# Graph kernel, edge part: the faded running total is written straight into the PSUM bank of the next sum

## The reference

```python
w_m = (efeat @ W_msg + b_msg).reshape(E, in_f, -1)      # E x 16 x 16
w_a = (efeat @ W_attn + b_attn).reshape(E, in_f, -1)
h_src = feat[src][:, :, None]
e1, e2 = w_m * h_src, w_a * h_src
seg_max = segment_max(e2, dst); ex = exp(e2 - seg_max[dst])
denom = segment_sum(ex, dst)
ft = segment_sum(e1 * (ex / denom[dst]), dst)
out = layernorm(x + ft.sum(axis=1))
```

## Time and profile before

| | us |
|---|---|
| median of 3 runs | 2380.55 |
| lowest, highest | 2374.79, 2388.63 |
| the profiled execution, device time | 2364.64 |
| its span, first to last instruction | 2362.8 |
| PE, DVE busy | 1745.0 (74%), 1722.0 (73%) |
| ACT, POOL busy | 1480.9 (63%), 1336.1 (57%) |
| mean granted clock of PE | 0.822 |

### The profile page before, as it was taken

How to read it: one execution, slowest core, us unless ns; L and a number is a source line. 1 busy time by engine, 2 the same in 40 slices (tenths; PEclk the granted TensorE clock), 3 DMA queues, 4 the chain that set the end, 5 groups by cost and what they waited for, 6 DMA issues and landing times.

```text
span 2362.8 us, 32949 instructions
## 1 busy us (share of the span) xinstructions
PE 1745.0 (74%) x5902; PEld 767.4 (32%) x5902; DVE 1722.0 (73%) x2102; ACT 1480.9 (63%) x5073; POOL 1336.1 (57%) x1556
## 2 busy tenths in 40 slices
PE   0566668950188888888878788888888888888845
PEld 0354442330033333333333333333333333333312
DVE  3576653120278898888879798889888888888956
ACT  5468830110367777777767677777777777777742
POOL 4234415445656666666666566666666666666640
PEclk9855569875589889888878898989888998889977
DMA  3010001001010000000000000000000000000000
GB/s 44 21 30 0 0 2 26 12 13 19 8 10 10 10 10 10 10 10 11 9 9 8 9 10 11 9 10 10 10 10 10 10 11 9 9 10 10 10 4 8
DMA packets 84286, 26.53 MB, mean 11 GB/s; under 512 B 62108, under 2 KB 80908, under 8 KB 84125
## 3 DMA queue, kind: packets, MB, share of 16 engines
q0 software_dynamic: 37232, 19.73, 6.9%
q1 hardware_dynamic: 43645, 5.60, 1.5%
q10 hardware_dynamic: 3376, 0.83, 0.2%
HBM read 23.46 MB, written 2.51 MB: 11 GB/s over the span
## 4 chain that ended last, share of the span: by engine, by line
issue 28%; PE 26%; ACT 17%; DVE 8%; POOLq 6%; POOL 5%; DVEq 4%; another core or an unknown queue 4%; ACTq 2%; DMA 1%; SPq 0%
PE pair L875 14%; ACT eo L1137 13%; PE pw L862 6%; PE pair L871 3%; PE pt L844 3%; POOLq L602 1%; ACT eo L1126 1%; DVE top L1588 1%; POOLq L580 1%; DVEq L1661 1%; POOL shared L553 1%; DVE rden L1637 1%; POOL place_records L585 1%; DVE eo L1573 1%
## 5 line engine op out<-in xcount | busy, mean ns | idle before, releaser
L659 POOL DMA_INDIRECT nbr<-table,rec x928 | 953.2, 1027 | 547.7 <-ACT eo L1137 285.7
L1137 ACT ACTIVATE eo<-pw,nbr 128x32 f32<-128x32 f32 x3712 | 728.0, 351 | 248.7 <-issue 243.5
L875 PE MATMUL pair<-eo,ident 128*128 128x512 f32 x1856 | 864.9, 621 | 2.7 <-DVE eo L1619 1.8
L875 PEld LDWEIGHTS pair<-eo,ident 128*128 128x128 f32 x1856 | 378.0, 205 | 529.7 <-issue 529.5
L1573 DVE TENSOR_TENSOR eo<-pw,nbr 128x1024 f32 (+1 forms) x348 | 408.1, 1218 | 88.6 <-remote 37.4
L862 PE MATMUL pw<-wk,termsT 100*128 100x512 bf16 x928 | 331.6, 448 | 158.5 <-issue 132.8
L844 PE MATMUL pt<-identb,terms 128*100 128x128 bf16 x928 | 102.6, 239 | 250.1 <-DVE terms L1561 134.8
L1619 DVE TENSOR_TENSOR eo<-eo (+1 forms) x232 | 272.6, 1215 | 1.9 <-ACT eo L1126 1.7
L1610 DVE TENSOR_TENSOR eo<-eo,bank 128x2048 f32 (+1 forms) x116 | 265.4, 2288 | 8.7
L1126 ACT ACTIVATE eo<-eo 128x2048 f32<-128x2048 f32 x116 | 220.1, 1898 | 46.6 <-DVE eo L1610 44.7
L1113 ACT CAST termsT<-pt 100x512 bf16<-100x512 f32 x232 | 134.3, 579 | 140.0 <-issue 50.5
(11 more groups left out here) (237 smaller groups left out, 1670.2 us busy)
## 6 DMA issues: line engine op xcount, KB each, us to landing
nbr<-table,rec POOLq DMA_INDIRECT x928
rec<-unit_recs SPq DMA_DIRECT2D x116, 8.0 KB
attr<-in_edge_attr_dram,rec POOLq DMA_INDIRECT x116
unit_recs<-place SPq DMA_DIRECT2D x27, 64.0 KB, 1.6
shared<-key_row SPq DMA_DIRECT2D x1, 1600.0 KB, 6.5
place<-in_src_dram,at_i POOLq DMA_INDIRECT x26, 2.6
shared<-sd_row ACTq DMA_DIRECT2D x1, 416.0 KB, 4.4
shared<-in_dst_dram,place POOLq DMA_INDIRECT x25
```

The source lines that it names most:

```text
L659: pool.indirect_dma_start(nbr[:, b, j * FEAT:(j + 1) * FEAT], None, table, bass.IndirectOffsetOnAxis(ap=rec[:, b, j:j + 1], axis=0)).then_ ...
L875: mm = pe.matmul(total, ident[:], eo[:, ring, j * 2 * CH:(j + 1) * 2 * CH], start=False, stop=(j == SLOT - 1), skip_group_check=True)
L1137: done = act.activation(eo[:, ring, lo:lo + wide], pw[:, j - 4, c * wide:(c + 1) * wide], ACT.Copy, scale=nbr[:, held, j * FEAT + c:j * FE ...
```

## The change

`acc` goes. `accumulate` writes the faded total into the bank of the coming sum (`into`, the other half of `pair`), and the eight products add to what stands there; `sums` has no product of its own for it, and its waits stay. So that the products add rather than overwrite, two marker products write both banks once, ahead of the loop; DVE waits for them (`s_marked`), sets the first bank to zero and gives the first `s_accd`.

```diff
--- before.py
+++ after.py
@@ -229,7 +229,6 @@
         top2 = sb("top2", [P, 2 * CH])
         top1 = sb("top1", [P, CH])
         mdiff = sb("mdiff", [P, CH])
-        acc = sb("acc", [P, 2 * CH])
         fade = sb("fade", [P, CH])
         rden = sb("rden", [P, CH])
         ratio = sb("ratio", [P, CH])
@@ -345,6 +344,7 @@
         s_p = sem("s_p")
         s_sum = sem("s_sum")
         s_accd = sem("s_accd")
+        s_marked = sem("s_marked")
         s_var = sem("s_var")
         s_std = sem("s_std")
         s_ft = sem("s_ft")
@@ -868,7 +868,6 @@
                 if half == 0:
                     pe.wait_ge(s_accd, seen + 1)
                     pe.sem_inc(s_settled_pe, 1)
-                    pe.matmul(total, ident[:], acc[:], start=True, stop=False, skip_group_check=True)
                 pe.wait_ge(s_p, seen * 2 + half + 1)
                 pe.sem_inc(s_settled_pe, 1)
                 for j in range(4 * half, 4 * half + 4):
@@ -879,6 +878,9 @@
 
             pe.wait_ge(s_wk, 16 * (TERMS + 4))
             pe.wait_ge(s_stage, 1)
+            for v in range(2):
+                mm = pe.matmul(pair[:, v, :], identb[0:KROWS, :], wk[:], start=True, stop=True)
+            mm.then_inc(s_marked, 1)
             for half in range(2):
                 turn(0, half, 0)
             for u in range(3):
@@ -1189,7 +1191,7 @@
             dve.memset(counts[:, NG * DPAD:NG * DPAD + DTAIL], 0.0)
             dve.memset(plane_at[:], 0.0)
             for s in (*s_full_free, *s_agg_free, *s_lin, *s_lin_free,
-                      s_g3_free, s_accd):
+                      s_g3_free):
                 dve.sem_inc(s, 1)
             dve.sem_inc(s_split, NCH)
             dve.sem_inc(s_g3, 2)
@@ -1535,7 +1537,6 @@
 
                 dve.wait_ge(s_over, 1)
                 dve.memset(terms[:, :, :, TERMS * FEAT:KROWS], 1.0).then_inc(s_ones, 1)
-                dve.memset(acc[:], 0.0)
                 dve.memset(pen[:, 0:1], -3e38)
                 dve.memset(pen[:, 1:2], 0.0)
                 dve.memset(bank[0][:], 0.0)
@@ -1543,8 +1544,9 @@
             layernorm(x1, y3, 1, clear)
             dve.drain().then_inc(s_x1, 1)
 
-            dve.memset(pair[:, 1, :], 1.0)
             dve.drain().then_inc(s_stage, 1)
+            dve.wait_ge(s_marked, 1)
+            dve.memset(pair[:, 0, :], 0.0).then_inc(s_accd, 1)
             step = dve.alloc_register("dve_step")
 
             def rest_one(unit, held, seen):
@@ -1618,12 +1620,12 @@
                     here = message(ring, 4 * half, 4 * half + 4)
                     dve.tensor_tensor(here, here, attention(ring, 4 * half, 4 * half + 4), ALU.mult).then_inc(s_p, 1)
 
-            def accumulate(unit, seen):
+            def accumulate(unit, into, seen):
 
                 dve.wait_ge(s_fade, seen + 1)
                 dve.wait_ge(s_sum, seen + 1)
                 dve.sem_inc(s_settled_dve, 1)
-                dve.tensor_tensor(acc[:].rearrange("p (c m o) -> p c m o", m=2, o=FEAT),
+                dve.tensor_tensor(pair[:, bass.ds(into, 1), :].rearrange("p r (c m o) -> p (r c) m o", m=2, o=FEAT),
                                   pair[:, bass.ds(unit, 1), :].rearrange("p r (c m o) -> p (r c) m o", m=2, o=FEAT),
                                   fade[:].rearrange("p (c o) -> p c o", o=FEAT)
                                   .unsqueeze(2).broadcast_to([P, FEAT, 2, FEAT]), ALU.mult).then_inc(s_accd, 1)
@@ -1687,7 +1689,7 @@
                 if ahead > 2:
                     rest_two(odd, v + 3)
                     scaled(third, third, v + 2)
-                accumulate(odd, dve.snap(v - 1, min_val=0, max_val=MANY))
+                accumulate(odd, even, dve.snap(v - 1, min_val=0, max_val=MANY))
                 weighted(here, v)
                 if load is not None:
                     dve.reg_mov(units, dve.value_load(levels[0:1, bass.ds(load, 1)], min_val=1, max_val=E))
```

## The result

The changed kernel takes 2414.76 us, median of 4 runs (2406.71 to 2422.37), against 2377.67 us before (4 runs, 2369.35 to 2388.63). The ratio is 1.0153, with a 95% interval of 1.0093 to 1.0213. It is slower by 37 us, just beyond the end of my range and on the side of the clock rival.

A forecast was written before the change was run, and what follows sets the result against it. Of 93 edge units, 61 were taken as bound by ScalarE's cast, 21 by VectorE at tile ends, 11 by TensorE. Terms of -5 + 7 + 0 = +2 us gave 2382 us, no change; range 2340 to 2412 us.

The forecast's parts named there:

- clock rival: Hole ahead of the sums brings the clock back later than some 5 us behind accumulate: about 2412 us; 25%.
- 1, the product leaves: Removing the acc product takes 194 us off TensorE, but only 14 of 116 units gain 0.35 us each: -5 us.
- 2, the clock: Hole ahead of the sums makes them 1 us later; half is paid in 14 units TensorE bounds: +7 us.
- 3, VectorE's write into PSUM: In accumulate, writing PSUM in place of SBUF: 0, within -1 to +1 us over 116 units.
- 4, waits: In the loop no wait is added; accumulate and the sums wait as before.
- 5, the start: Ahead of the loop, two marker products and VectorE's wait for them are hidden in its 67.25 us of idle time.
- ScalarE rival: ScalarE's scaled copies beside the sums lose 0.4 us of idle time in 92 units: about 2344 us; 27%.
- full product on the path: In all units the removed product's whole 194 us leaves the path: 2186 us; 2%.
- What I said the profile would show: Edge part: sums 1.1 to 1.3 us behind accumulate, records over 617 ns, clock under 0.87, some 60 cast waits.

The follow-up runs named there:

- experiment 1: The changed kernel with a product of zeros, 512 columns wide, at the removed product's old place ahead of the sums: ratio 0.9973 to the kernel before.
- experiment 5: Last of the eight products of the sums left out: ratio 0.9992 in the changed kernel, 1.0036 in the kernel before.
- Experiment 2: The changed kernel with a product of zeros at the removed product's place, narrowed from 512 columns: ratio 1.0004 with 256 columns, 1.0141 with one.

## Why the prediction was wrong

Forecast "no change", measured +1.5%. Taken by its own steps:

- **1, the product leaves.** 1.67 us per unit and the start of the sums at 1.1 to 1.3 us behind accumulate were right (1.27 us; 1.6 to 1.7 on average in ordinary units before, 2.1 behind a tile's end). Wrong was the count of the units that TensorE bounds. I got 93 - 61 - 21 = 11 by taking the waits for ScalarE's cast in one trace as if they left nobody else, but the second and third traces of the kernel before have 32 and 50 such waits in place of 61, and the timelines of the three give 17, 29 and 22 units of some 79.
- **2, the clock. This is the step that failed, in both of its terms: how much later the sums are, and who pays.** I took 1 us more for the sums, nearest to the middle between 0 and the 1.75 us of the earlier trace rows, less the 0.35 us of step 1. Measured: 1.5 us more on average (9.0 for 7.5 us), 1.7 us in the unit at 1859.60 and 2.8 us in the one at 1888.87 (9.92 for 7.11 us). Net of the earlier start, the sums end 1 us later (9.1 to 10.1 us behind accumulate's end), not 0.65. What I had as the bad unit of the earlier trace rows became the usual one. I set the lower end by the earlier trace rows, where a hole of 1.01 us did no harm; but there it lay behind the sums. The new one lies ahead of them, behind a phase that already has holes (0.58 us just before it at 1857.87). That this is why it harms is my reading; the runs show only that it does.
- **And in who pays.** I charged half of it to 14 units, and gave no reason for the half; to the others I gave 2.6 us of slack from one unit. That was one of the roomiest: of the quiet ordinary units of that trace, 3 of 55 have 5.5 us or more between the sums' end and the next accumulate, and on average it is 4.3 us, which is 1.3 us of slack. The units behind a tile's end had nearly none before the change (3.1 to 3.3 us from the sums' end to the next accumulate, where 3.0 is the shortest), and they pay nearly all of it.
- By the table, means of three traces each: the 24 units behind a tile's end go from 13.56 to 14.38 us, +20 us; the 24 that end a tile from 15.68 to 15.53, -4 us. In these the later sums leave their last products a high clock (0.59 us a pair at 1884.83, where 1538.11 before had 1.01); that this is the gain is argued. The 68 ordinary ones go from 13.75 to 13.94, +13 us, and the stalled part adds 55 - 39 = 16 us, but both vary by more than that from one execution to the next. So the table places 16 of the 37 us firmly. Where the rest lies stays open, though experiment 1 shows that it goes with the product too.
- **3, VectorE's write into PSUM, 4, waits, and 5, the start** were right: 690 ns against 679, ratio 0.997 with all of them in; and VectorE's idle stretch ahead of the first attributes is still 65.34 us.
- **The rivals.** The clock rival had the mechanism, the sign and nearly the time (2412 for 2415). It got 25%: I held against it that the clock came back within the sums in every unit I had read. It does, but too late: its condition was later than some 5 us behind accumulate, and the measured mean is 5.2 to 5.3 us. That its time came out so near is partly luck, since its sum was off in its terms: it priced a third of the 92 units that end no tile at 0.9 us more, where the 24 behind a tile's end pay 0.8 us and ordinary ones little. The ScalarE rival's time (2344 us) didn't come. Whether its wait for the cast shrank can't be told from 22.3 to 58.9 us against 33.3 to 86.9. The full product on the path is refuted by the result itself, since the product left and the time rose; experiment 5 puts one product of eight in the changed kernel at 25 to 38 us of 116 x 0.86 = 100 us.
- **What I said the profile would show** held for the start, the mean record and the clock (0.84 for 0.87). It didn't for the cast (39 waits in place of some 60), but that sign was no use: the kernel before has 32 and 50 in its other traces.

The Trainium skill (TensorE: Matmul & The Clock Gate, Part 1) says that activity releases the throttle. I cited it and gave it too little weight. Experiment 2 agrees with it: the same instructions with 512 columns keep the time (0.9973) and with one column they don't (1.0141).

No kernel here that computes the whole result beats the one before. The zero product, 0.9973 (0.9927 to 1.0019), can't be told from it.

## What to carry to other kernels

Before a product is taken off TensorE, look at what stands on both sides of it. If the engine waits for something else there anyway, the product may cost nothing and be what keeps the clock up for the long products behind it; here one product, moved from ahead of the sums to behind them, made 3.5%. Price a hole at what the products behind it cost in the trace's worst unit, and pay it in every unit whose slack is smaller, from a table of all units and not from one timeline. Seeding the accumulation from VectorE was free in itself here (690 for 679 ns, ratio 0.9973 with it in). I would expect a gain from it only where TensorE is busy up to that point; no run here shows one.

## What was unexpected of the hardware

- The clock can fall behind a hole rather than in it: at 1858.00 to 1859.60 it is 1.00 with 0.46 us of work in 1.60, and in the dense sums right behind it 0.63. So it went in 25 to 44 of the 56 or 57 ordinary units of each trace of the changed kernel; behind a tile's end it was mostly low already (0.68 at 1887.00 to 1889.00).
- A product of one column per unit, with both its weight loads, leaves the sums as slow as no product (723 ns, ratio 1.0141); with half the columns they are nearly as fast as with all (640 for 616 ns).
- Fewer products needn't save time: with seven in the kernel before, the sums' mean record went up from 617 to 635 ns, and the ratio is 1.0036 (0.9988 to 1.0083).
- Several engines at once stand idle for 1 to 8 us in some units, in every kernel, for 15 to 75 us in all. Executions of the same kernel differ in it (15, 65 and 37 us before), and the profile names no releaser for it.
